# Normalising each self-attention unit in two halves on GpSimd, with TensorE's transposes waiting for each half

## The chip, the cores and the metric

The kernel runs on one core of one Trainium2 chip. The metric is the device time of one execution in microseconds (us). Engines are named as the profile names them: PE is TensorE (PEld its weight loads), DVE is VectorE, ACT is ScalarE, POOL is GpSimd, and SP is the engine that issues the DMAs.

## The reference

A decoder block on x of shape (4, 256, 256): windowed causal self-attention with rotary embedding, cross-attention on a 64-wide context, and a gated feed-forward whose hidden values are kept two out of four.

```
x = x + self_attention(layernorm(x))      # 32 query heads, 8 key heads, 64 wide, window 32 back, causal
x = x + cross_attention(layernorm(x), ctx) # 16 heads, 16 wide, causal
x = x + ffn(layernorm(x))                  # silu(x wg) * (x wu), the 2 largest of each 4 kept, times wd
self_attention: softmax(q k^T / 8, masked) v, then wo
```

The change touches only one step of this: in the self-attention's softmax, the division of the exponentials by their row sums.

## The kernel before

The work goes batch by batch (B = 4), and each engine has its own program in which the order is written out by hand; engines meet at semaphores only. All of the activations of a batch stay on chip.

The self-attention of a batch is cut into NQB = 8 units of 32 query rows each; a unit has all 32 heads at once, as a tile `prob` of 128 rows (4 heads that share a key head, times 32 queries) by 512 columns (8 key heads, times a window of 64 keys). After them come 12 cross-attention units in the same buffers (4 of four heads, 8 of two), so that a batch has UNITS = 20 units. `prob` has ND = 4 buffers, and unit i uses buffer i % 4.

A self unit goes through these steps: PE makes the scores (`unit_scores`, L502 and L505); DVE takes the row maxima (L926) and subtracts them (L930); ACT takes the exponential (L1271); DVE sums the rows (L940) and takes the reciprocals (L946), which increments `s_inv`; POOL multiplies the 128x512 tile by the reciprocals, each of which is spread over 64 columns (`unit_norm`, L1173), and increments `s_norm` by one; PE transposes the tile in four pieces of 128 columns into one PSUM bank (`unit_transpose`, L544); ACT copies the result to SBUF as `pT` (L1289); PE multiplies by the values (`unit_values`, L565), and ACT copies the output away (`unit_out`, L1296, which increments `s_oT`).

The loop of PE over a batch's self stage runs i from 3 to 11: scores of unit i (while i < 8), transposes of unit i - 3, from i = 8 on one piece of the output projection (`window_out`, L604, eight matmuls of 256 columns; in the last batch two pieces at i = 8), then the values of unit i - 4. At i = 8 PE therefore goes from the values of unit 3 straight to the transposes of unit 5. Scores of units 0 to 2 are made ahead, at the end of the batch before. At i = 11 PE also transposes the next batch's normalised rows (`transpose_norm`, L462), between the transposes and the projection.

DVE's loop is, for each i, maxima and subtraction of unit i, then sums and reciprocals of unit i - 1. POOL's program of the self stage is the eight `unit_norm` and nothing between them, except in batch 0: there `split_weights` (L1179, the low parts of the feed-forward's weights) stands behind each of units 4 to 7. Then POOL takes the inverse roots of the layer norms (`inverse_root`, L1149), on which DVE's `normalise` (L883) waits.

The waits at the edited places: PE waits for `s_norm` at u + 1 before the first of a unit's four transposes, and then for the PSUM bank (`wait_pT`); DVE waits for `s_norm` of the unit four back before it overwrites its reciprocals.

Of the kernel before, what the change touches and what calls it, by code (L numbers as in the profile page):

```python
# [20 lines left out]
ALU = mybir.AluOpType  # L21
# [6 lines left out]
P = 128  # L28
# [8 lines left out]
NQB = S // QB  # L37
# [21 lines left out]

V_SECOND = V_BLOCKS - 2 * 16  # L60
ND = 4
NPT = 4
HEAD = 3

# [51 lines left out]
def cross_heads(j):  # L116

    if j < XU0:
        return [HPT * (j // 2) + j % 2 + 2 * k for k in range(4)]
    j -= XU0  # L120
    return [HPT * (j // 4) + 4 * (j % 2) + j // 2 % 2 + 2 * k for k in range(2)]


def build(nc, x, ctxT, wqk, wv, wo, xwq, xwk, xwv, xwo, wgu, wd, trig, masks, ident, rowmask, out):
    es = ExitStack()
    with es:
        def sb(name, shape, dt=F32):
            return es.enter_context(nc.sbuf_tensor(name, shape, dt))

        def sem(name):  # L130
            return es.enter_context(nc.semaphore(name))
# [45 lines left out]

        prob = sb("prob", [P, ND, 512])
        mask_f = prob[:, 0, 0:2 * WK + P]

        warm = prob[:, 1, 0:P]
        mx = sb("mx", [P, ND, 8])
        total = sb("total", [P, ND, 8])
        inv = sb("inv", [P, ND, 8])
        pT = sb("pT", [P, NPT, 512])

# [76 lines left out]
        s_norm = sem("s_norm")  # L263
# [41 lines left out]
        def wait_drained(eng, name, b):  # L305

            k, n = ring_use(name, b)
            eng.wait_ge(s_drained[k], n + 1)

        def wait_pT(eng, u):  # L310

            k = u - UNITS * (B - 1) - NQB
            if 0 <= k < XU0:
                eng.wait_ge(s_pTv, k + 1)
            else:
                eng.wait_ge(s_pT, u + 1 - (XU0 if k >= XU0 else 0))
# [126 lines left out]
        def _(pe):  # L443
# [85 lines left out]
            def ffn_banks_free(b):  # L529

                for use in (FFN_USES[:4] if b - 1 == HELD else FFN_USES)[-NF:]:
                    wait_drained(pe, use, b - 1)

            def unit_transpose(b, i):
                u = UNITS * b + i
                pe.wait_ge(s_norm, u + 1)
                if b and i < 2:
                    ffn_banks_free(b)
                if b == B - 1 and NQB <= i < NQB + 2:
                    wait_drained(pe, f"gate1{i - NQB}", HELD)  # L540
                if u >= 2:
                    wait_pT(pe, u - 2)
                for c in range(4):
                    mm = pe.transpose(ps[:, BANK_PT + i % 2, c * P:(c + 1) * P],  # L544
                                      prob[:, i % ND, c * P:(c + 1) * P], ident_sb[:])
                mm.then_inc(s_tr, 1)

            def unit_values(b, i):
                u = UNITS * b + i
                wait_pT(pe, u)  # L550
                pT_i = pT[:, i % NPT, :].rearrange("p (c n) -> p c n", c=4)
                if i == (0 if b else P // QB):
# [17 lines left out]
            def cross_values(b, units):  # L570
# [13 lines left out]
                for kt in range(tile + 1):  # L584
                    for i in units:
                        pT_i = pT[:, i % NPT, :].rearrange("p (c n) -> p c n", c=4)
                        for k, h in enumerate(cross_heads(i - NQB)):
# [272 lines left out]
        def _(dve):  # L860
# [52 lines left out]
            def unit_shape(i):  # L913
                return dict(g=8 if i < NQB else (4 if i - NQB < XU0 else 2))

            def unit_max(b, i):
# [6 lines left out]
                if i >= NQB:  # L923
                    dve.tensor_reduce(mx[:, i % ND, 0:g], src, AX.X, ALU.max, negate=True).then_inc(s_max, 1)  # L924
                    return
# [8 lines left out]
            def unit_sum(b, i):  # L934

                u = UNITS * b + i
                g = unit_shape(i)["g"]
                dve.wait_ge(s_exp, u + 1)
                if i < NQB:
                    dve.tensor_reduce(total[:, i % ND, 0:g],  # L940
                                      prob[:, i % ND, :].rearrange("p (g k) -> p g k", g=g),
                                      AX.X, ALU.add).then_inc(s_sum, 1)
                    dve.wait_ge(s_sum, NQB * b + i + 1)
                if u >= ND:
                    dve.wait_ge(s_norm, u - ND + 1)
                dve.reciprocal(inv[:, i % ND, 0:g], total[:, i % ND, 0:g]).then_inc(s_inv, 1)  # L946

            def chunk_values(b, c, j):
# [55 lines left out]
            def unit_pT(b, i):  # L1004
                u = UNITS * b + i
                dve.wait_ge(s_tr, u + 1)
                dve.wait_ge(s_av, u - NPT + 1)
                dve.tensor_copy(pT[:, i % NPT, :], ps[:, BANK_PT + i % 2, :]).then_inc(s_pTv, 1)

# [133 lines left out]
        @block.gpsimd  # L1143
        def _(pool):
            def inverse_root(which, n, tiles=range(TT)):

                for t in tiles:
                    pool.wait_ge(s_var, TT * (n - 1) + t + 1)
                    pool.tensor_tensor(rstd[:, which, t:t + 1], vareps[:, which, t:t + 1], power[:],  # L1149
                                       ALU.pow).then_inc(s_rstd, 1)  # L1150

            def rope_sums(name, b, n):

                g = int(name[1:])
                if b is None and name[0] == "q" and g in SWAPPED:
                    pool.wait_ge(s_swapped, SWAPPED.index(g) + 1)
                else:
                    wait_drained(pool, name, b)
                t = rope[:, (n - 1) % 2]
                if name[0] == "q":  # L1160
                    to = qs[:, 2 * (g // R):2 * (g // R) + 2, :, g % R, :]
                    cos, sin = (t[:, k].rearrange("p c (u s) -> p c u s", s=QB) for k in (0, 1))
                else:
                    to = cos = t[:, 0]
                    sin = t[:, 1]
                pool.tensor_tensor(to, cos, sin, ALU.add).then_inc(s_sums, 1)  # L1166

            def unit_norm(b, i):
                u = UNITS * b + i
                g = 8 if i < NQB else (4 if i - NQB < XU0 else 2)  # L1170
                pool.wait_ge(s_inv, u + 1)
                p = prob[:, i % ND, :].rearrange("p (g k) -> p g k", g=g)
                pool.tensor_tensor(p, p, inv[:, i % ND, 0:g].unsqueeze(2).broadcast_to([P, g, 512 // g]),  # L1173
                                   ALU.mult).then_inc(s_norm, 1)

            def split_weights(c):

                pool.wait_ge(s_whi, c + 1)
                pool.tensor_tensor(lo_c[c], raw[:, c, :], hi_c[c].bitcast(F32), ALU.subtract)\  # L1179
                    .then_inc(s_wlo, 1)  # L1180

            def next_group(b, name, k):
                rope_sums(name, b, RG * (b + 1) + k)

            def batch(b, more):
                for i in range(NQB):
                    unit_norm(b, i)
                    if b == 0 and i >= LATE:
                        split_weights(i - LATE)
                if more:  # L1190
                    inverse_root(0, 3 * b + 2)
                if b == 0:
                    for c in range(NQB - LATE, WCHUNKS):
                        split_weights(c)
                n = 3 * b + (3 if more else 2)
                inverse_root(1, n, (0,))
                inverse_root(1, n, (1,))
                if more:
                    next_group(b, "k0", 1)
                    next_group(b, "k1", 2)  # L1200
                for i in range(XU + LAG_V):
                    if 1 <= i <= XU:
                        unit_norm(b, NQB + i - 1)
                    if i in X_FILL and more:
                        next_group(b, f"q{X_FILL[i]}", 3 + X_FILL[i])
                    if i == OUT0_AT + 1:
                        inverse_root(2, n + 1, (0,))
                if more:
                    next_group(b, "q6", 9)
                inverse_root(2, n + 1, (1,))  # L1210
                if more:
                    next_group(b, "q7", 10)

            pool.memset(power[:], -0.5).then_inc(s_power, 1)
            pool.memset(vb[:, 0, 0], 0.0)
            pool.memset(k4[:, 0:2].bitcast(F32), 0.0)
            pool.wait_ge(s_power, 1)
            inverse_root(0, 1)
            pool.wait_ge(s_xn, TT)
            pool.memset(k4[:, 2:].bitcast(F32), 0.0).then_inc(s_zero, 1)  # L1220
            for g in range(GROUPS):
                rope_sums(f"k{g}", None, g + 1)
            for g in range(QG):
                rope_sums(f"q{g}", None, GROUPS + g + 1)
            for b in range(B):
                batch(b, b + 1 < B)

        @block.scalar
        def _(act):
# [54 lines left out]
            def unit_pT(b, i):  # L1284
                u = UNITS * b + i
                act.wait_ge(s_tr, u + 1)
                if u >= NPT:
                    act.wait_ge(s_av, u - NPT + 1)
# [191 lines left out]
```

## Time and profile before

| | |
|---|---|
| median of 3 runs | 413.85 us (413.63 to 414.40) |
| the profiled execution's own time | 414.07 us |
| its span, first to last instruction | 412.3 us |
| mean granted TensorE clock | 0.996 |
| PE busy | 391.8 us, 95% |
| DVE, ACT, POOL busy | 287.1, 209.0, 160.0 us |

The span is 1.8 us shorter than the time of the same execution, for what lies before the first and behind the last instruction. "Busy" counts only the time of instructions; an engine at 95% can still stall for the rest, and which stalls matter is read from the chain of work that ended last and from the timeline.

### The profile page before, as it was taken

What the parts mean: (1) busy time and instruction counts of PE and PEld (TensorE: products, weight loads), DVE (VectorE), ACT (ScalarE), POOL (GpSimd) and SP (SyncE); (2) the same over time, 40 slices, a digit from 0 to 9 for tenths busy, and PEclk for the clock granted to TensorE, in tenths of its full rate; (3) what the DMA queues carried; (4) which work ended last, traced back from release to release, by engine and by line L of the source; (5) the groups of instructions that cost most, each with busy time, mean ns of one, the idle gap of its engine ahead of it and who ended that gap; (6) DMA issues with size and microseconds to landing.
All of it is one profiled execution on the core that took longest, in us unless ns stands there. A gap on an engine that the chain in (4) does not pass through costs nothing.

```text
span 412.3 us, 8020 instructions
## 1 busy us (share of the span) xinstructions
PE 391.8 (95%) x2967; PEld 316.0 (77%) x2968; DVE 287.1 (70%) x611; ACT 209.0 (51%) x534; POOL 160.0 (39%) x160
## 2 busy tenths in 40 slices
PE   8997999899999999999999999999999999978996
PEld 7676778667699777777789877877788879746895
DVE  4977931788769972788849974588958965565373
ACT  1574731487334841387453752287634835368230
POOL 5562790478411420367610440167732500156000
PEclk9999999999999999999999999999999999989999
DMA  7995420313001300243000400232001300210000
GB/s 221 350 325 147 139 84 27 110 34 82 3 6 52 103 0 27 79 109 91 2 6 2 155 0 2 99 106 72 1 2 54 100 2 17 88 53 0 27 2 25
DMA packets 33446, 28.90 MB, mean 70 GB/s; under 512 B 18688, under 2 KB 28032, under 8 KB 33152
## 3 DMA queue, kind: packets, MB, share of 16 engines
q1 hardware_dynamic: 33408, 28.40, 22.3%
q8 instruction: 24, 0.39, 0.4%
q14 instruction: 14, 0.11, 0.1%
HBM read 19.21 MB, written 5.24 MB: 59 GB/s over the span
## 4 chain that ended last, share of the span: by engine, by line
PE 63%; DVE 18%; issue 6%; ACT 5%; POOL 4%; DMA 2%; SPq 1%; POOLq 0%; DVEq 0%; ACTq 0%
PE ps L604 13%; PE ps L472 11%; PE ps L544 8%; PE ps L671 7%; PE ps L687 3%; PE ps L590 3%; DVE mx L926 3%; PE ps L565 3%; PE ps L481 3%; POOL prob L1173 3%; ACT prob L1279 2%; DVE total L940 2%; DVE rope L896 2%; PE ps L524 2%; PE ps L643 2%
## 5 line engine op out<-in xcount | busy, mean ns | idle before, releaser
L1173 POOL TENSOR_TENSOR prob<-prob,inv 128x512 f32<-128x512 f32 x80 | 83.0, 1043 | 84.1 <-DVE inv L946 84.0
L472 PE MATMUL ps<-xnT,wqk_sb 128*128 128x256 f32 x320 | 77.4, 384 | 0.7 <-DVE rope L896 0.4
L472 PEld LDWEIGHTS ps<-xnT,wqk_sb 128*128 128x128 f32 x320 | 57.8, 190 | 11.2 <-issue 4.6
L1279 ACT ACTIVATE prob<-ps,mx 128x128 f32<-128x128 f32 (+1 forms) x128 | 52.7, 428 | 19.2 <-DVE mx L924 18.1
L1166 POOL TENSOR_TENSOR qs<-rope 128x512 f32<-128x512 f32 x32 | 40.8, 1274 | 43.0 <-DVE rope L896 39.0
L544 PE MATMUL ps<-ident_sb,prob 128*128 128x128 f32 x320 | 49.8, 280 | 4.7 <-POOL prob L1173 4.7
L1289 ACT ACTIVATE pT<-ps 128x512 f32<-128x512 f32 x76 | 45.3, 600 | 12.3 <-PE ps L544 12.0
L896 DVE TENSOR_TENSOR rope<-ps,trig_sb 64x512 f32<-64x512 f32 x70 | 48.2, 688 | 0.9
L544 PEld LDWEIGHTS ps<-ident_sb,prob 128*128 128x128 f32 x320 | 37.6, 142 | 12.8 <-POOL prob L1173 8.1
L1149 POOL TENSOR_TENSOR rstd<-vareps,power 128x1 f32<-128x1 f32 x24 | 13.2, 555 | 77.8 <-DVE vareps L875 77.5
L924 DVE TENSOR_REDUCE mx<-ps 128x2 f32<-128x512 f32 (+1 forms) x48 | 32.7, 690 | 12.5 <-PE ps L524 11.7
L505 PEld LDWEIGHTS ps<-kd,qs 128*128 128x128 f32 x256 | 33.8, 192 | 1.3
L505 PE MATMUL ps<-kd,qs 128*128 128x128 f32 x256 | 33.7, 275 | 0.0
L1271 ACT ACTIVATE prob<-prob 128x512 f32<-128x512 f32 x32 | 20.2, 631 | 25.7 <-DVE prob L930 25.5
L671 PE MATMUL ps<-x_hi,wgu_hi 128*128 128x256 f32 x128 | 32.2, 285 | 0.3 <-ACT x_hi L1386 0.3
L671 PE MATMUL ps<-x_hi,wgu_lo 128*128 128x256 f32 x128 | 31.5, 280 | 0.0
L604 PE MATMUL ps<-wo_sb,first_out 128*128 128x256 f32 x128 | 30.1, 379 | 0.0
L604 PE MATMUL ps<-wo_sb,qs 128*128 128x256 f32 x128 | 29.4, 379 | 0.0
L893 DVE TENSOR_TENSOR rope<-ps,trig_sb 128x512 f32<-128x512 f32 x35 | 23.9, 684 | 6.6 <-PE ps L472 5.3
L1279 ACT ACTIVATION_READ_ACCUMULATOR prob<-ps,mx 128x1 f32 x128 | 27.2, 213 | 0.0
L604 PEld LDWEIGHTS ps<-wo_sb,qs 128*128 128x128 f32 x128 | 23.7, 190 | 4.2 <-issue 1.4
L687 PE MATMUL ps<-wd_sb,work 128*128 128x256 f32 x112 | 26.2, 380 | 0.2 <-DVE work L970 0.2
(147 smaller groups left out, 694.8 us busy)
## 6 DMA issues: line engine op xcount, KB each, us to landing
k<-kx SPq DMA_DIRECT2D x32, 128.0 KB, 2.9
q<-qx SPq DMA_DIRECT2D x32, 128.0 KB, 2.6
vb<-v_sb SPq DMA_DIRECT2D x42, 64.0 KB, 2.1
wqk_sb<-in_wqk SPq DMA_DIRECT2D x4, 512.0 KB, 6.7
work<-in_wgu SPq DMA_DIRECT2D x4, 512.0 KB, 8.7
wo_sb<-in_wo SPq DMA_DIRECT2D x1, 2048.0 KB, 14.3
vb<-v_sb SPq DMA_DIRECT2D x36, 32.0 KB, 3.2
wd_sb<-in_wd SPq DMA_DIRECT2D x1, 1024.0 KB, 5.7
```

The source lines that it names most:

```text
L472: mm = pe.matmul(o[:, half, :], wqk_sb[:, k, g, half, :], xnT[:, 0, k, :], start=(k == 0), stop=(k == KT - 1))
L505: mm = pe.matmul(o[:, p * P:(p + 1) * P], qs[:, p, i].rearrange("p r s -> p (r s)"), kd[:, p, :, i * QB:i * QB + WK], start=False, stop=(p ...
L544: mm = pe.transpose(ps[:, BANK_PT + i % 2, c * P:(c + 1) * P], prob[:, i % ND, c * P:(c + 1) * P], ident_sb[:])
L604: mm = pe.matmul(half_banks(use, b)[:, 0, :], window_o[t][:, pair, r, :], wo_sb[:, pair, r, :], start=(pair == 0 and r == 0), stop=(pair = ...
L671: mm = pe.matmul(half_banks(use, b)[:, m, :], wp[:, k, w, c * 4 + 2 * j + m, :], xp[:, k, :], start=(n == 0), stop=(xp is x3_lo and k == K ...
L687: mm = pe.matmul(half_banks(*use)[:, t, :], hidden[b][c][:, j, t * P:(t + 1) * P], wd_sb[:, c * 4 + j, :], start=((apart or not c) and t = ...
L896: ins = dve.tensor_tensor(t[at:at + 64, 1], src[here], trig_sb[here, 1:2, :].broadcast_to([64, 2, S]), ALU.mult)
L924: dve.tensor_reduce(mx[:, i % ND, 0:g], src, AX.X, ALU.max, negate=True).then_inc(s_max, 1)
L1166: pool.tensor_tensor(to, cos, sin, ALU.add).then_inc(s_sums, 1)
L1173: pool.tensor_tensor(p, p, inv[:, i % ND, 0:g].unsqueeze(2).broadcast_to([P, g, 512 // g]), ALU.mult).then_inc(s_norm, 1)
L1279: ins = act.activation(prob[:, i % ND, h * k:(h + 1) * k], ps[:, BANK_S + i % 2, h * k:(h + 1) * k], ACT.Exp, bias=mx[:, i % ND, h:h + 1], ...
L1289: act.activation(pT[:, i % NPT, :], ps[:, BANK_PT + i % 2, :], ACT.Copy).then_inc(s_pT, 1)
```

## The change

POOL multiplies a self unit in two instructions of 128x256 (key heads 0 to 3, then 4 to 7), each of which increments `s_norm`. PE waits for the first before the transposes of columns 0 to 255, and for the second between the second and the third transpose. A cross unit stays one instruction, which increments `s_norm` by two. The other wait on `s_norm`, that of DVE, counts accordingly.

```diff
+NORMS = 2
@@ unit_transpose (PE)
-                pe.wait_ge(s_norm, u + 1)
+                pe.wait_ge(s_norm, NORMS * u + (1 if i < NQB else NORMS))
@@
                 for c in range(4):
+                    if c == 2 and i < NQB:
+                        pe.wait_ge(s_norm, NORMS * (u + 1))
                     mm = pe.transpose(ps[:, BANK_PT + i % 2, c * P:(c + 1) * P],
                                       prob[:, i % ND, c * P:(c + 1) * P], ident_sb[:])
@@ unit_sum (DVE)
-                    dve.wait_ge(s_norm, u - ND + 1)
+                    dve.wait_ge(s_norm, NORMS * (u - ND + 1))
@@ unit_norm (POOL)
-                pool.tensor_tensor(p, p, inv[:, i % ND, 0:g].unsqueeze(2).broadcast_to([P, g, 512 // g]),
-                                   ALU.mult).then_inc(s_norm, 1)
+                if i >= NQB:
+                    pool.tensor_tensor(p, p, inv[:, i % ND, 0:g].unsqueeze(2).broadcast_to([P, g, 512 // g]),
+                                       ALU.mult).then_inc(s_norm, NORMS)
+                    return
+                for half in range(NORMS):
+                    at = slice(g // NORMS * half, g // NORMS * (half + 1))
+                    pool.tensor_tensor(p[:, at], p[:, at], inv[:, i % ND, at].unsqueeze(2)
+                                       .broadcast_to([P, g // NORMS, 512 // g]), ALU.mult).then_inc(s_norm, 1)
```

## Rows read from the trace of the kernel before

**Rows 1.** The page: engines' busy time, and the chain that ended last by engine.
```profile
PE 391.8 (95%) x2967; PEld 316.0 (77%) x2968; DVE 287.1 (70%) x611; ACT 209.0 (51%) x534; POOL 160.0 (39%) x160
PE 63%; DVE 18%; issue 6%; ACT 5%; POOL 4%; DMA 2%; SPq 1%; POOLq 0%; DVEq 0%; ACTq 0%
```
**Rows 2.** Waits, whole run: us in total, times, longest us.
```profile
PEld ps L544 <- POOL prob L1173: 8.1, 15, 0.9
PE ps L544 <- POOL prob L1173: 4.7, 10, 0.7
```
**Rows 3.** The same view of PE alone: batch 0's self stage, 32 to 64 us.
```profile
PE ps L544 <- POOL prob L1173: 1.9, 3, 0.7
```
**Rows 4.** The same view, batch 2's self stage, 222 to 245 us.
```profile
PE ps L544 <- POOL prob L1173: 0.6, 2, 0.5
```
**Rows 5.** The chain in batch 2: start us, us, what.
```profile
236.97 0.21 DVE inv L946
237.18 0.07 issue
237.25 1.05 POOL prob L1173
238.31 0.04 issue
238.35 0.66 PE ps L544 x4
239.01 1.73 PE ps L604 x8
```
**Rows 6.** Timeline, batch 2, unit 5: start us, us, engine, line, tiles, count, idle before.
```profile
237.22 0.42 PEld L565 LDWEIGHTS ps<-pT,vb 64*64 64x64 f32 x16 [0.17 <-issue]
...
237.96 0.60 ACT L1296 ACTIVATE first_out<-ps 128x512 f32<-128x512 f32 x1
...
238.35 0.66 PE L544 MATMUL ps<-ident_sb,prob 128*128 128x128 f32 x4 [0.46 <-POOL prob L1173]
...
238.84 1.89 PE L604 MATMUL ps<-wo_sb,first_out 128*128 128x256 f32 x8
...
239.36 2.04 POOL L1173 TENSOR_TENSOR prob<-prob,inv 128x512 f32<-128x512 f32 x2 [1.07 <-DVE inv L946]
```
**Rows 7.** Busy time by stretch, batch 2's units 3 to 7 on DVE.
```profile
228.64:239.87 11.23, 10.62 (x125) 8.79 (x125) 10.86 (x22) 8.90 (x15) 5.73 (x6) 1.00 0.34 101
```
**Rows 8.** The line that normalises: ns shortest/median/longest, first and last start.
```profile
L1173 POOL TENSOR_TENSOR prob<-prob,inv x80: 1037/1043/1052, 37.0 to 378.7; 128x512 f32<-128x512 f32 x80
```
**Rows 9.** POOL's groups by shape, 0 to 12 us: busy us, mean ns.
```profile
L1149 POOL TENSOR_TENSOR rstd<-vareps,power 128x1 f32<-128x1 f32 x2 | 1.1, 554 | 1.2 <-DVE vareps L875 1.1
L1215 POOL MEMSET vb<- 128x256 f32 x1 | 0.3, 313 | 0.0
...
L1214 POOL MEMSET power<- 128x1 f32 x1 | 0.1, 99 | 0.3 <-POOLq L1471 0.3
```
**Rows 10.** Timeline, PE: two transposes behind a stall, and what follows.
```profile
385.92 0.44 PE L462 MATMUL ps<-ident_sb,xn 128*128 128x128 f32 x2
386.20 0.60 PE L715 MATMUL ps<-trig_sb,ident_sb 128*128 128x256 f32 x2
```
**Rows 11.** Timeline, PE: passages with and without waits between instructions, batches 0 and 2.
```profile
58.07 0.66 PE L462 MATMUL ps<-ident_sb,xn 128*128 128x128 f32 x4
...
241.76 1.89 PE L604 MATMUL ps<-wo_sb,first_out 128*128 128x256 f32 x8
...
243.58 0.67 PE L565 MATMUL ps<-pT,vb 64*64 64x128 f32 x16
```
**Rows 12.** Timeline, batch 0: POOL's queue around unit 5, and what waits on it.
```profile
47.00 1.27 POOL L1179 TENSOR_TENSOR wgu_lo<-work,wgu_hi 128x512 fp32r<-128x512 f32 x1
...
48.23 1.05 POOL L1173 TENSOR_TENSOR prob<-prob,inv 128x512 f32<-128x512 f32 x1
...
49.33 0.66 PE L544 MATMUL ps<-ident_sb,prob 128*128 128x128 f32 x4 [0.58 <-POOL prob L1173]
...
54.91 1.08 POOL L1149 TENSOR_TENSOR rstd<-vareps,power 128x1 f32<-128x1 f32 x2
...
55.51 1.87 DVE L883 TENSOR_SCALAR xn<-x_buf,moments,rstd 128x256 f32<-128x256 f32 x2 [3.14 <-POOL rstd L1149]
```
**Rows 13.** DVE's groups in batch 2, 228.64 to 239.87 us: busy us, mean ns.
```profile
L930 DVE TENSOR_TENSOR prob<-ps,mx 128x512 f32<-128x512 f32 x5 | 3.5, 692 | 0.2
```

## The prediction

> **What bounds the kernel now.** The page comes first: PE is busy for 95% of the span and the chain that ended last runs through it for 63%; POOL, the engine that gets more instructions, holds 4% of that chain [rows 1]. The change can therefore gain only where PE stands still for POOL's multiplication, and the view of waits sizes that: 4.7 us on PE's matmuls in ten places [rows 2]. That is a ceiling for removing the waits whole, and not all of them are in self units or on the path. By stage: three waits with 1.9 us in batch 0 and two with 0.6 us in batch 2; batches 1 and 3 have two each [rows 3, 4].
>
> The chain tells which of them count. In batch 2 it goes from DVE's reciprocals of unit 5 (ended 237.18) through POOL's multiplication (237.25 to 238.30) to the transposes of unit 5 at 238.35 and on through the projection [rows 5]. The timeline shows why: PE's weight loads for the values of unit 3 had ended at 237.64, and its matmuls stood idle 0.46 us [rows 6]. The other wait of the stage is at unit 1. It is paid out of slack: DVE is busy 10.86 of 11.23 us from unit 3 on [rows 7], so DVE sets when unit 5's reciprocals are there, and PE, if it passes unit 1 earlier, waits longer at unit 5. So one place per batch counts, four in all, and at each what matters is when the last of the four transposes is through.
>
> **What a place is worth, PE's side.** Today the four transposes start 0.05 us behind POOL's end, at 238.35, and the next matmul starts at 238.84: 0.49 us [rows 6]. With halves the first two run while POOL is in the second half (the first is there about 0.6 us behind 237.25, and the second takes some 0.5 us more, enough for two transposes), and only two stand behind its end. A row shows just that: two transposes behind a stall, with the next matmul 0.28 us after their start [rows 10]. The saving is 0.49 - 0.28 = 0.21 us, less whatever the two halves take longer than the whole. Call that d.
>
> **d, POOL's side.** A whole takes 1.043 us, between 1.037 and 1.052 in all 80 [rows 8]. Two in a row take 2.04 us, so the second starts 0.046 us ahead of the first one's end [rows 6]. If an instruction has a fixed part f and the rest goes by columns, then two halves take 1.043 + f - 0.046, so d = f - 0.046. No row has a multiplication of 256 columns, so f is bounded. From below: a memset of one column takes 0.099 us [rows 9]; it reads nothing, so a multiplication's f is hardly less, d >= 0.053, and a gain from the split itself is excluded. From above: the power of one column takes 0.554 us [rows 9], d = 0.51; most of that should be the power itself. I take f = 0.15, d = 0.10: near the memset, which is the same path without operands, with something added for two input streams.
>
> First what the rows show: the whole is 1.043 us for 512 columns, and the add with two full operands is not faster. The Trainium skill (GPSIMD Engine Reference, section 3.1) gives 4497 ns for a tensor_tensor add of 2048 fp32 columns, which stands with no row here. An estimate from that page's figure and a 1.27 us subtraction of 512 columns in this trace [rows 12] is f = 0.2 us, by which d would be 0.154 and the sum below a gain of 0.07 us instead of 0.34.
>
> **Batches 1 to 3.** Each place gives 0.21 - 0.10 = 0.11 us, 0.33 us together. Next late would be ACT's copy of unit 3's output, for which the projection waits: it ends at 238.56 [rows 6], 0.28 us ahead of 238.84, so it doesn't bind at 0.11, the less as PE passes unit 3 earlier. Behind the place PE runs without a stall to the end of the stage, so I count the 0.11 through to the end; what follows on DVE, ACT and the DMAs starts from PE's results and moves along. In the last batch the same place stands before two pieces of the projection and is worth the same. Units 6 and 7 get their multiplications at 239.36 in a row [rows 6], d and 2d later, and are transposed only behind a piece of projection each (1.9 us): no cost. The inverse roots behind them come 0.2 us later; DVE's normalise is followed there by waits for ACT and PE, so I cost it at nothing; without this cover it would be 0.2 us a batch.
>
> **Batch 0.** Here POOL has a queue: the split of weights from 47.00, and unit 5's multiplication right behind it at 48.23 [rows 12]. Unit 4's halves push the split back by d, unit 5's by another d, so the place is worth 0.21 - 0.20 = 0.01 us. Unit 6 and 7 come 3d and 4d late, then the inverse roots (54.91), then normalise, which ends at 57.38 [rows 12]; its reader on PE, the transposes at 58.07 [rows 11], has 0.69 us less what is 0.4 us late: covered at d = 0.10, used up from about d = 0.16. The waits of unit 0 and 1 in this batch are slack as in the others.
>
> **The added wait on PE.** 32 of them. Where the second half is there already, the wait stands alone before one transpose. The transposes of the next batch's rows have just this pattern, two, a wait, two: 0.66 us for the four [rows 11], as the four of a unit without it [rows 12]. I take nothing. Behind the waiting transpose are queued the projection and the values; nobody else waits for more than these. DVE's wait counts two per unit and is for a unit four back, long done. Cross units do what they did.
>
> **Sum.** 0.33 + 0.01 = 0.34 us gained. Against the profiled execution's 414.07 (span 412.3, 1.77 around it) that is 413.73; that execution lies 0.22 above the median of the runs shown, so against 413.85 it is 413.5 us. In general the gain is 3 x (0.21 - d) + (0.21 - 2d) = 0.84 - 5d: 0.57 us at the lower bound of f, nothing at d = 0.168 (f = 0.214). This kernel's time can be told from no change at about 0.2%, 0.83 us; the sum can't reach that for any d above zero.
>
> **Rivals.**
> - The fixed part is large, and POOL becomes the bound in batch 0. Speaking for it: 0.554 us for one column [rows 9]. Against: it is a power. At f = 0.554, d = 0.51: batches 1 to 3 lose 0.30 each, batch 0's place 1.02 - 0.21 = 0.81, and normalise, 2.04 late, ends at 59.42 when PE wants it at 58.07 + 0.81 + 0.28: another 0.3. Sum 2.0, so 415.9 us. It decides the sign from f = 0.214 and is beyond 0.2% slower from f = 0.38.
> - The inserted wait costs PE issue time. For it: from the projection's eight matmuls to the values, with two waits between, 1.82 us pass where eight of 0.216 take 1.73, so 0.09 us for that passage [rows 11]. At units 6, 7 and a third one of each batch that PE paces: 12 x 0.09 = 1.1, net of 0.34 it is 414.6 us. Against: the row with the same pattern shows none.
> - PE, not DVE, paces the units from 1 to 5, and what is saved at unit 1 (and at unit 0 and 1 of batch 0) counts too: four to five more times 0.11, 413.0 us. Against: DVE is busy all through [rows 7].
> - POOL's second half is held up by DVE. The 80 multiplications spread over 15 ns beside a DVE that hardly pauses [rows 7, 8], so nothing holds a whole one today; but two instructions open a gap into which one of DVE's, some 0.69 us long [rows 13], could get. If each place lost that once, 0.69 - 0.11 in four places, 2.3 us: 416.2. The Trainium skill (SBUF — State Buffer, "Who interferes with whom") has such an exclusive lock, for a DVE instruction with two SBUF inputs or in a two-port mode; DVE's maxima, subtraction and sums here have at most one SBUF tensor beside PSUM or are reductions, so by that rule it would not happen, and the trace agrees with that.
> - The change does nothing measurable because unit 5's place is lost to something else that is late: 413.85, inside the forecast's own band.
>
> **Chances.** Forecast, a small gain or nothing (413.2 to 414.0): 0.70. Large fixed part 0.10, wait on PE 0.08, more places count 0.08, held-up halves 0.04. The range has to take in d from 0.053 to about 0.25, a shift of 413.3 to 414.3, the cases at 413.0 and 414.6, and a quarter of a microsecond for runs that differ: 412.9 to 414.8. Faster by over 0.2% needs the third rival and luck: 0.10. Slower by over 0.2% is the first and the fourth rival, with half of the second: 0.16. Within: 0.74.
>
> **What the profile of the changed kernel would show.** 64 multiplications of 256 columns; their mean and the start of the second behind the first give d directly (0.57 us each if f = 0.10, 0.60 if 0.15, 0.80 if 0.55). At unit 5 of a batch two transposes run, a gap of about 0.2 us, then two more, and the projection starts about 0.11 us earlier behind DVE's reciprocals than today's 1.67 (237.18 to 238.84). DVE's rows between units 3 and 7 keep their spacing. In batch 0 the split of weights starts d later. Wrong would be: halves longer than 0.8 us, a normalise on which PE waits at the end of batch 0's stage, transposes of units 6 and 7 spread wider than 0.66, or DVE pausing for PE between units 3 and 7.

## The result: 1% slower

| | before | changed |
|---|---|---|
| executions, us | 413.63, 413.85, 414.40, 415.50 | 417.21, 417.82, 420.25, 420.27 |
| median, us | 414.12 | 419.03 |
| profiled execution (span), us | 414.07 (412.3) | 417.21 (415.4) |

The ratio is 1.0104, 95% interval 1.007 to 1.0139. The changed kernel's executions form two groups: in the two near 417.5 us the mean granted TensorE clock is 0.996, in the two at 420.3 it is 0.988. The profiled one belongs to the first, so its trace holds 3.1 us of the loss; the other 3 us are taken up with the first experiment.

Where the 3.1 us are, the waits of TensorE in batch 0's self stage say at once. The changed kernel, 32 to 66 us (us in total, times, longest); the kernel before has 1.9 us in three waits on POOL there [rows 3] and none on `xn`:

```profile
PE ps L464 <- DVE xn L887: 3.1, 1, 3.1
PE ps L548 <- POOL prob L1183: 0.8, 3, 0.4
```

The waits that the change was to shorten have shrunk, from 1.9 to 0.8 us. A wait of 3.1 us for VectorE's normalise has appeared. Its place in the timeline of the changed kernel (start us, us, engine, line):

```profile
55.56 1.08 POOL L1153 TENSOR_TENSOR rstd<-vareps,power 128x1 f32<-128x1 f32 x2
...
56.16 5.53 DVE L887 TENSOR_SCALAR xn<-x_buf,moments,rstd 128x256 f32<-128x256 f32 x2 [3.69 <-POOL rstd L1153]
56.60 4.95 POOL L1189 TENSOR_TENSOR wgu_lo<-work,wgu_hi 128x512 fp32r<-128x512 f32 x4
...
58.23 0.44 PE L464 MATMUL ps<-ident_sb,xn 128*128 128x128 f32 x2
...
61.75 0.44 PE L464 MATMUL ps<-ident_sb,xn 128*128 128x128 f32 x2 [3.08 <-DVE xn L887]
```

The inverse roots come 0.65 us later than in [rows 12]: four late pairs make 0.56 of it (0.14 each, below), and the two programs start 0.1 us apart. But the two normalises behind them, 1.87 us together before [rows 12], now take 5.53. Taken one by one, the second of them is the whole of it. The kernel before:

```profile
55.51 0.41 DVE L883 TENSOR_SCALAR xn<-x_buf,moments,rstd 128x256 f32<-128x256 f32 x1 [3.14 <-POOL rstd L1149]
...
56.03 1.35 DVE L883 TENSOR_SCALAR xn<-x_buf,moments,rstd 128x256 f32<-128x256 f32 x1
```

and the changed kernel:

```profile
56.68 5.01 DVE L887 TENSOR_SCALAR xn<-x_buf,moments,rstd 128x256 f32<-128x256 f32 x1
```

In both kernels it starts 0.08 us behind GpSimd's first weight split (55.95 before, 56.60 now), where the same instruction takes 0.41 us undisturbed. The first split of the kernel before:

```profile
55.95 1.28 POOL L1179 TENSOR_TENSOR wgu_lo<-work,wgu_hi 128x512 fp32r<-128x512 f32 x1
```

Before, the normalise ended 0.15 us behind the first split (57.38 against 57.23); now it ends 0.15 us behind the fourth (61.69 against 56.60 + 4.95 = 61.55). TensorE's transposes of the second tile of rows wait for it.

It is not the only one that is held. Of the 24 normalises in the trace of the kernel before, 19 take 0.40 to 0.42 us. The other five all overlap an instruction of GpSimd: the one above (1.35), one of 1.12 us beside a multiplication of `prob` in the last batch, and three of 1.46 to 1.47 us beside an addition of the rotary embedding, such as this:

```profile
105.59 1.46 DVE L883 TENSOR_SCALAR xn<-x_buf,moments,rstd 128x256 f32<-128x256 f32 x1
...
105.64 1.26 POOL L1166 TENSOR_TENSOR qs<-rope 128x512 f32<-128x512 f32 x1 [0.60 <-DVE rope L896]
```

Here the normalise is shown as starting first, by 0.05 us, and is held all the same. TensorE never waited for any of the five. The four others are the same in the changed kernel.

The Trainium skill (SBUF — State Buffer, "Who interferes with whom") lets a tensor_scalar in a two-port mode and a GpSimd instruction exclude each other for the whole instruction. The trace agrees that the normalise is held; that it is held through four instructions in a row, 5.01 us, is more than the page says. In which mode the normalise runs, no run here shows.

What was costed in the prediction is there too. GpSimd's groups by shape, whole run of the changed kernel (busy us, mean ns, then idle time before them):

```profile
L1183 POOL TENSOR_TENSOR prob<-prob,inv 128x256 f32<-128x256 f32 x64 | 38.2, 620 | 62.3 <-DVE inv L950 62.3
L1178 POOL TENSOR_TENSOR prob<-prob,inv 128x512 f32<-128x512 f32 x48 | 49.7, 1040 | 19.9 <-DVE inv L950 19.2 <-issue 0.4
```

The halves' shortest, median and longest time, in ns:

```profile
L1183 POOL TENSOR_TENSOR prob<-prob,inv x64: 612/612/1061, 37.0 to 333.1; 128x256 f32<-128x256 f32 x64
```

The longest, 1.06 us, is a single one; what held it is told with the rivals below.

And unit 5 of batch 2 in the changed kernel's timeline, the answer to [rows 5, 6]:

```profile
240.36 0.20 DVE L950 RECIPROCAL inv<-total 128x8 f32<-128x8 f32 x1
...
240.65 1.18 POOL L1183 TENSOR_TENSOR prob<-prob,inv 128x256 f32<-128x256 f32 x2 [0.93 <-DVE inv L950]
...
241.31 1.01 PE L548 MATMUL ps<-ident_sb,prob 128*128 128x128 f32 x4
241.88 0.20 PEld L548 LDWEIGHTS ps<-ident_sb,prob 128*128 128x128 f32 x2 [0.37 <-POOL prob L1183]
...
242.16 1.89 PE L608 MATMUL ps<-wo_sb,first_out 128*128 128x256 f32 x8
```

Two transposes, a gap of 0.37 us on the weight loads, two more. From the start of the reciprocals to the projection it is 1.80 us, against 238.84 - 236.97 = 1.87 before: 0.07 us gained. Batches 1 and 3 show the same two times to 0.01 us. The pair takes 1.18 us against 1.04, so d is 0.14.

### The profile page after: what moved, and what is told of

Same layout as the page of the kernel before. It is cut to its first block, busy times and chain, and to the rows that moved or that the text cites. A ratio compares the mean times of both kernels' runs of the same rounds, so it can differ in the third digit from the quotient of the medians.

```text
span 415.4 us, 8101 instructions
## 1 busy us (share of the span) xinstructions
PE 394.2 (95%) x2968; PEld 316.7 (76%) x2968; DVE 290.8 (70%) x611; ACT 208.7 (50%) x534; POOL 164.6 (40%) x192
## 4 chain that ended last, share of the span: by engine, by line
PE 66%; DVE 16%; POOL 5%; ACT 5%; issue 5%; DMA 1%; SPq 1%; POOLq 0%; DVEq 0%; ACTq 0%
PE ps L608 12%; PE ps L474 11%; PE ps L675 8%; PE ps L548 7%; PE ps L691 4%; PE ps L594 3%; PE ps L483 3%; PE ps L507 3%; PE ps L569 3%; POOL prob L1183 3%; ACT prob L1289 2%; DVE mx L930 2%; DVE rope L900 2%; PE ps L526 2%; DVE total L944 2%
## 5 line engine op out<-in xcount | busy, mean ns | idle before, releaser
L1183 POOL TENSOR_TENSOR prob<-prob,inv 128x256 f32<-128x256 f32 x64 | 38.2, 620 | 62.3 <-DVE inv L950 62.3
L1178 POOL TENSOR_TENSOR prob<-prob,inv 128x512 f32<-128x512 f32 x48 | 49.7, 1040 | 19.9 <-DVE inv L950 19.2
L548 PE MATMUL ps<-ident_sb,prob 128*128 128x128 f32 x320 | 51.6, 281 | 2.8 <-POOL prob L1183 1.1
L887 DVE TENSOR_SCALAR xn<-x_buf,moments,rstd 128x256 f32<-128x256 f32 x24 | 18.4, 765 | 13.0 <-POOL rstd L1153 12.4
```

Of the source, the lines that this page charges most:

```text
L1183: pool.tensor_tensor(p[:, at], p[:, at], inv[:, i % ND, at].unsqueeze(2) .broadcast_to([P, g // NORMS, 512 // g]), ALU.mult).then_inc(s_no ...
```

## The experiments

Theory A: the loss is one event in batch 0, the second normalise held behind the row of splits, and the clock that falls after it. Rival B: it is spread over pairs and waits. Rival C: it is only the longer queue of GpSimd. The letters D to G in later expectations stand for narrower questions, told there.

**1. Halves in batch 0 alone.**
```diff
-                if i >= NQB:
+                if i >= NQB or b > 0:
```


> Halves in batch 0 alone; batches 1 to 3 normalise in one instruction as before. Theory A (one event: in batch 0 the second normalise of the next batch's rows, on VectorE, is held up until all four of GpSimd's last weight splits are through, and TensorE stalls 3.1 us for it): the whole loss is here, 417 to 420 us, with a normalise of about 5 us and a stall of about 3 us before the transposes of the next batch's rows. Theory B (the loss is spread: every pair of halves and every added wait costs a little): a quarter of it, about 415 us, and no normalise longer than 1.5 us.

Measured: 419.58 us median; executions 420.25, 415.32, 420.70, 418.90. The wait for `xn` is 3.1 us. TensorE's added waits stand in all batches here. The whole loss is here, so B falls. This trace is also one with the low clock. Busy time by stretch; the column behind POOL's busy time is the granted clock, 0.50 being the 1.2 GHz level and 1.00 the 2.4 GHz one:

```profile
58.00:62.00 4.00, 0.92 (x18) 0.51 (x18) 3.96 (x1) 0.60 (x1) 3.81 (x4) 0.86 0.00 0
62.00:64.00 2.00, 1.99 (x6) 1.71 (x7) 0.00 (x0) 0.60 (x1) 0.00 (x0) 0.50 0.42 125
64.00:66.00 2.00, 2.00 (x5) 1.10 (x4) 0.00 (x0) 0.00 (x0) 0.00 (x0) 0.50 0.02 6
66.00:68.00 2.00, 2.00 (x19) 1.33 (x19) 1.19 (x4) 0.60 (x1) 0.48 (x1) 0.58 0.00 0
```

TensorE is busy 0.92 of the 4 us from 58 to 62. The clock falls inside the stall, at 60.8, and comes back at 67.7: 6.8 us at the lower level. Its span is 418.5 us where the changed kernel's profiled one is 415.4, with the same stall. In the latter the clock stayed up:

```profile
55.00:62.00 7.00, 3.92 (x48) 2.85 (x41) 5.42 (x2) 1.75 (x3) 6.54 (x7) 1.00 0.01 4
62.00:66.00 4.00, 4.00 (x30) 2.62 (x29) 1.28 (x5) 1.19 (x2) 0.55 (x1) 1.00 0.21 66
```

So the same stall costs 3 us, or 6 with such a spell. There are cases between: the profiled executions of experiments 5 and 9, 418.57 and 418.40 us, have the lower clock for 3.4 us only, just behind the stall. What decides between the three isn't shown. The execution of 415.32 us (clock 0.992) has no room for a stall of 3 us: executions of the kernel before at that clock take 415.0 to 415.7. One in four seems to have escaped; it has no trace.

**2. Halves in batches 1 to 3 alone.**
```diff
-                if i >= NQB:
+                if i >= NQB or b == 0:
```


> Halves in batches 1 to 3 alone; batch 0 as before. Theory A: no loss, the three places give 0.07 us each (1.87 to 1.80 us from the reciprocals of unit 5 to the projection), 413.7 to 414.0 us beside 413.9 of before. Theory B: three quarters of the loss, 416 to 418 us.

Measured: 414.20 us median, ratio 1.0013 (0.9981 to 1.0044). Nine of ten executions lie between 413.54 and 415.28; one is at 419.67 with a clock of 0.988. The two normalises of batch 0 take 1.87 us in the profiled one, and the three places 1.80 us each. The median lies above the 413.7 to 414.0 expected, but the kernel before had 414.26 in this series. As A says, with a warning: batch 0 is here that of the kernel before, and once in ten it seems to have lost as well; that execution has no trace.

**3. The changed kernel, the four splits behind both normalises.**
```diff
                 if b == 0:
+                    pool.wait_ge(s_xn, 2 * TT)
                     for c in range(NQB - LATE, WCHUNKS):
```


> The changed kernel with one more wait: in batch 0 GpSimd starts its last four weight splits only when VectorE has normalised both tiles of the next batch's rows. Theory A, contention between these two: both normalises take 0.41 us, the stall of 3.1 us before the transposes is gone, the splits end about 0.6 us later, and the time is that of before, 413.5 to 414.5 us. Theory C (the loss is GpSimd's queue that has become longer, not who holds whom): the wait lengthens that queue further, so the time stays at 417 us or rises to 418.

Measured: 414.12 us median of ten (413.46 to 415.08), ratio 0.9990 (0.9978 to 1.0001). The timeline:

```profile
56.51 0.93 DVE L887 TENSOR_SCALAR xn<-x_buf,moments,rstd 128x256 f32<-128x256 f32 x2 [3.71 <-POOL rstd L1153]
57.52 4.96 POOL L1189 TENSOR_TENSOR wgu_lo<-work,wgu_hi 128x512 fp32r<-128x512 f32 x4 [0.53 <-DVE xn L887]
...
58.58 0.66 PE L464 MATMUL ps<-ident_sb,xn 128*128 128x128 f32 x4
```

Both normalises take 0.93 us, and the four transposes run in one go. GpSimd's queue has become longer, the loss is gone: C falls. This run is also the change without its accident. The gain that the prediction's formula gives with the measured d, 0.14 us, is what the medians differ by (414.12 against 414.26), but the interval includes no gain at all: by time it isn't shown.

**4. The kernel before with the same wait.** The same line added.

> The kernel before with the same added wait. Theory A: in the kernel before one normalise of the same pair already took 1.35 us, hidden behind the projection; with the wait it takes 0.41 us and the time stays within 0.3 us of before, with less spread between executions (before: 413.63 to 415.5). Theory C: slower than before by what the splits end later, about 0.6 us.

Measured: 414.38 us, ratio 1.0006 (0.9994 to 1.0018), normalises 0.93 us. The hold of one split in the kernel before cost nothing, and taking it away brings nothing; the spread between executions stayed too (413.95 to 415.50), so that part of the expectation was wrong.

**5 and 6. The kernel before, whole units, GpSimd delayed in batch 0,** by four single columns, and by eight.
```diff
+                if b == 0:
+                    for k in range(4):
+                        pool.tensor_tensor(hold[:, k:k + 1], power[:], power[:], ALU.mult)
                 if more:
                     inverse_root(0, 3 * b + 2)
```


> The kernel before, nothing halved; in batch 0 GpSimd multiplies four times a single column ahead of the inverse roots, about 0.6 us if one costs the fixed part of 0.15 to 0.2 us, which is as late as the halves made it. Theory D (the delay alone makes the second normalise lose its place to all four splits): a normalise of 5 us, a stall of 3.1 us and 417 to 420 us. Theory E (it is a race that the delay leaves as it is, and the halves change by more than the time at which they end): most executions as before, 413.9 to 414.5.

> The same with eight single columns, about 1.2 us of delay. Theory D: the stall is there too, 417 to 421 us. Theory E: as before, unless a normalise held by one split ends too late for TensorE: 57.4 + 1.2 = 58.6 against 58.07 is a stall of 0.5 us, 414.5 us.

Measured: 418.48 us (417.31 to 419.64) and 420.84 us (419.72 to 421.48). All eight executions show the loss; the stalls in the profiled ones are 3.2 and 3.8 us. The first one's timeline:

```profile
54.94 0.65 POOL L1193 TENSOR_TENSOR hold<-power 128x1 f32<-128x1 f32 x4
55.52 1.09 POOL L1150 TENSOR_TENSOR rstd<-vareps,power 128x1 f32<-128x1 f32 x2
56.12 5.57 DVE L884 TENSOR_SCALAR xn<-x_buf,moments,rstd 128x256 f32<-128x256 f32 x2 [3.78 <-POOL rstd L1150]
```

Nothing is halved, and the loss is there: the halves matter here only as 0.6 us of delay. The rows also price what the prediction had to bound, a multiplication of one column: four follow each other in 0.65 us, each taking 0.215 and starting 0.145 behind the one before (0.18 to 0.19 us each in experiments 6, 9 and 10).

**7. As 3, but TensorE waits for both halves first.**
```diff
-                pe.wait_ge(s_norm, NORMS * u + (1 if i < NQB else NORMS))
+                pe.wait_ge(s_norm, NORMS * (u + 1))
-                    if c == 2 and i < NQB:
-                        pe.wait_ge(s_norm, NORMS * (u + 1))
```


> As the run with halves and the splits behind the rows, but TensorE waits for both halves before the first transpose. This measures what the inner wait is worth by itself. By the place's arithmetic the projection of unit 5 starts 1.80 + 0.21 = 2.01 us behind the reciprocals instead of 1.80, so 0.8 us in four batches: 414.9 us against 414.1. If the place were hidden behind something else, the time would stay at 414.1.

Measured: 414.88 us, 0.76 above the 414.12 of 3 (0.8 expected), though in another series; between the series the kernel before moved by 0.09. Against the kernel before of its own series it is 0.53 us more (ratio 1.0007, 0.9989 to 1.0026), about the 4 x 0.14 that the pairs take longer; the ratio alone can't tell it from no change. Batch 2, unit 5:

```profile
237.59 1.18 POOL L1181 TENSOR_TENSOR prob<-prob,inv 128x256 f32<-128x256 f32 x2 [0.93 <-DVE inv L948]
...
238.83 0.66 PE L546 MATMUL ps<-ident_sb,prob 128*128 128x128 f32 x4 [0.45 <-POOL prob L1181]
...
239.32 1.89 PE L606 MATMUL ps<-wo_sb,first_out 128*128 128x256 f32 x8
```

From the pair's start to the projection 1.73 us, against 242.16 - 240.65 = 1.51 with the inner wait: 0.22 us per place. Four such places make 0.88 us, and about that arrives in the time, so the place is not hidden behind anything.

**8. The changed kernel, batch 0's splits in another order.** GpSimd does all eight units, one split, the inverse roots, and (behind `s_xn`) six splits, an inverse root and the last split.

> The changed kernel with GpSimd's batch 0 in another order: all eight units, one split, the inverse roots, then (behind both normalises) six splits, the next inverse root, the last split. Units 5 to 7 no longer stand behind a split and no normalise runs beside one. Expected by contention theory: no normalise over 0.5 us, the wait of unit 5 in batch 0 falls to that of the other batches, 0.1 to 0.3 us less than the run with halves and a wait: 413.8 us. If the splits now end too late for the cross queries, slower instead: 415 us.

Measured: 414.21 us, ratio 0.9990 (0.9976 to 1.0003). Unit 5's wait in batch 0 shrank as expected (0.5 us in two waits instead of 0.8 in three), but 0.3 us came back as a wait on a later normalise, which runs beside the last split and takes 1.34 us, where none over 0.5 was expected; nor is the 413.8 us that was expected there. Not to be told from 3 or from the kernel before.

**9 and 10. Smaller delays:** one and two single columns in the place of four.

> The kernel before with one multiplication of a single column ahead of batch 0's inverse roots: about 0.15 us of delay. Theory F (a threshold: below some lateness the second normalise gets in behind the first of the four splits, above it behind the last): as before, 413.8 to 415.2, with a normalise of 1.35 us. Theory G (nothing but the fine phase between the two engines decides, and any shift may lose): some or all executions at 417 us and more already here.

> The same with two single columns, 0.3 us. Theory F: either as before or as with four (417 us and more), and not less affected than with one. Theory G: need not lie between its neighbours; a mixture of executions with and without the stall, each either below 415.5 or above 417.

Measured: 418.24 us (417.91 to 419.03) and 419.55 us (419.33 to 419.92). Even 0.15 us of delay brings the loss in all eight executions; the stalls in the two profiled ones are 2.8 and 3.0 us. If there is a threshold, it lies below 0.15 us.

**11. Two waits that are long fulfilled in the place of the delay.**
```diff
+                if b == 0:
+                    for k in range(2):
+                        pool.wait_ge(s_power, 1)
```


> The kernel before with two waits on a semaphore that was set at the start, on GpSimd ahead of batch 0's inverse roots: two more instructions in its stream, no more work. Theory F (lateness decides): as before, 413.8 to 415.2, second normalise 1.35 us. Theory G (any shift of the two engines against each other, or of the instruction stream, can lose): executions at 417 us and above with a normalise of 5 us.

Measured: 414.12 us, ratio 0.9983 (0.9964 to 1.0002), normalises 1.87 us in the profiled one, in none of ten executions a loss. Two more waits in the stream without work behind them don't do it. This speaks for lateness and against the stream.

**12. The changed kernel, two splits in a row instead of four;** the other two behind the next inverse root.

> The changed kernel with two weight splits behind the inverse roots of the next rows instead of four; the last two come behind the next inverse root, for which GpSimd has to wait anyway. If the normalise is held until the row of splits ends, it takes about 2 x 1.23 + 0.15 = 2.6 us instead of 5.0, ends near 59.3 and TensorE stalls 0.7 us at most instead of 3.1: 414.3 to 415.0 us. If it is held for a fixed time, or by anything but the splits, it stays at 5 us and the time at 417 us.

Measured: 414.95 us, ratio 1.0016 (0.9994 to 1.0037). The timeline:

```profile
56.01 3.10 DVE L887 TENSOR_SCALAR xn<-x_buf,moments,rstd 128x256 f32<-128x256 f32 x2 [3.71 <-POOL rstd L1153]
56.46 2.50 POOL L1189 TENSOR_TENSOR wgu_lo<-work,wgu_hi 128x512 fp32r<-128x512 f32 x2
...
59.16 0.44 PE L464 MATMUL ps<-ident_sb,xn 128*128 128x128 f32 x2 [0.66 <-DVE xn L887]
```

The hold ends with the row of splits, two or four, and the stall is 0.66 us as expected (0.7 at most). The normalise is held by the row and not for a time of its own. But a row need not hold it to its end: the other two splits of this run, also in a row (63.25 to 65.79), have a later normalise beside them, and it takes 1.35 us from 63.32, getting in behind the first.

**What stays open.** Why the normalise gets in behind the first split in the kernel before and only behind the last one when both come 0.15 us later. How far behind the first split it starts doesn't decide: the profiled executions have 0.07 to 0.08 us where it got in and 0.06 to 0.09 us where it didn't, and of experiments 1 and 2, with 0.07 us both, one lost and one did not. Nor is lateness more than a name for what the delays did, since the later row in 12 let the normalise in. The runs show how often (never in the kernel before, none of whose executions took more than 415.7 us, nor in 11, seemingly once in ten in 2, in three of four in 1, in all others with a delay and the four splits in a row) but not what decides.

## Why the prediction was wrong

Point by point:

- **What bounds the kernel, and the four places that count:** right. The places gained, at 0.07 us each in batches 1 to 3.
- **What the inner wait saves, 0.21 us:** right; 0.22 in experiment 7, 0.76 us over four batches. [rows 10], from which it came, marks no stall ahead of its two transposes, but behind the real one above the next matmul follows 0.28 us behind their start too (241.88 to 242.16).
- **d:** mis-sized. I took f = 0.15 and d = 0.10; measured are 0.61 us for a half, 1.18 for a pair, d = 0.14, and about 0.2 for a single column. The estimate that stood beside it from the Trainium skill (GPSIMD Engine Reference, section 3.1), f = 0.2 and d = 0.154, was the better one, in part by luck: it took the slope from two instructions with two full operands, while the multiplication costs (1.043 - 0.612) / 256 = 1.7 ns a column here, which with 0.612 for a half gives f = 0.18. By 0.84 - 5d the gain becomes 0.14 us instead of 0.34. This error is small.
- **Batch 0, the step that failed:** I read the two normalises in [rows 12] as 1.87 us of work that would move with the inverse roots, and found 0.69 us of cover for a delay of 0.4. With d = 0.14 that delay is 0.6, and by this step it was still covered. But 1.87 was no duration: it was 0.41 of work, a little gap and 1.35 us of an instruction held by GpSimd, beside a row of four splits that could hold it for 5 us. The question "what does it cost if it comes 0.4 us later" had the answer "between nothing and the rest of the row as well": 5.01 - 1.35 = 3.66 us more of hold, with 0.6 of delay and less 0.7 of cover 3.6 us at most. Measured is a stall of 3.08 us, before the third transpose and not the first. The prediction had this sign in its list of what would be wrong, a normalise on which PE waits at the end of batch 0's stage, but no price for it beyond 0.3 us.
- **The rivals:** the first had the right place, transposes of the next rows waiting for a late normalise, with the wrong size (0.3 us) and the wrong cause (a large f). The fourth had the cause, one engine holding the other, but looked only in one direction, VectorE holding GpSimd's halves inside the stage. GpSimd holding VectorE's normalise 7 us further on was in the rows and in neither. What the fourth rival describes did happen once, in the last batch, with a kind of VectorE instruction that it had not considered, a comparison of the feed-forward:

```profile
333.10 1.06 POOL L1183 TENSOR_TENSOR prob<-prob,inv 128x256 f32<-128x256 f32 x1
...
333.61 1.09 DVE L966 TENSOR_TENSOR work<-work 128x512 bf16<-128x512 f32 x1
```

The half takes 1.06 us instead of 0.61 and the comparison 1.09 instead of the 0.68 it takes in the kernel before. It is the second half of unit 7, transposed only at 337.85, so it cost nothing; experiments 2, 3 and 7 have the same one (1.06 us).
- **The inserted wait costs issue time, PE paces the units:** neither is seen; the transposes of units 6 and 7 take 0.66 us as before.
- **The clock:** not in the prediction. With the stall it makes up to half of the loss in part of the executions.

Accounted for the profiled execution: 3.08 for the stall, less three times 0.07, and 0.07 lost at batch 0's unit 5 (the projection follows the reciprocals by 49.98 - 47.92 = 2.06 us, before 49.82 - 47.83 = 1.99): 2.94 of 3.1 us. The rest is not placed; the two programs also start 0.1 us apart.

## What to carry to other kernels

When an instruction's time in a row is far above that of the same instruction elsewhere, it can be a wait that the profile shows as work: look at what runs beside it on the other engine, and take as its worst case the whole row of such neighbours, not the value seen. A change that makes a queue a few tenths of a microsecond longer has to be followed to whoever stands at its end, here 7 us and two engines away from the edit. Where GpSimd has a row of instructions that nobody waits for yet, one wait that lets VectorE's short instruction go first can be cheap; in experiments 3 and 4 it cost nothing that could be measured.

## What the runs showed of the hardware

A VectorE tensor_scalar of 128x256 that takes 0.41 us alone took 1.34 us beside a single GpSimd tensor_tensor of 128x512 (experiment 8), and 2.6 and 5.0 us beside two and four in a row (1.23 us apart) when it was held to the end of the row; beside other rows of two and four it took 1.35 us. A GpSimd multiplication by the reciprocals took 0.61 us for 256 columns and 1.04 for 512, one of a single column about 0.2; two of 512 in a row overlap by some 0.05 us. A TensorE stall of about 3 us came with no time, 3.4 us or 6.8 us at the lower clock in the profiled executions, the last worth 3 us of time.
